# Routed experts behind a graph attention: the expert stage with its up part one block further ahead

## What is computed

```python
x = x + gnn(layernorm(x), adj, W, a)          # 4 heads, softmax over neighbours
t = layernorm(x)                              # 8192 tokens x 128
scores = t @ Wg.T + bg; top 2 of 8 experts, p = softmax of the two scores
for e in range(8):
    h = relu(t @ W1[e].T + b1[e])             # 128 -> 512
    y = h @ W2[e].T + b2[e]                   # 512 -> 128
    out = out + combine[..., e:e+1] * y       # combine holds p, zero elsewhere
x = x + out
```

## Time and profile before

| | us |
|---|---|
| median of 3 runs | 859.47 (856.22 to 861.64) |
| span of the profiled execution | 856.6 |
| busy over the span: TensorE, VectorE, ScalarE, GpSimd | 647.1, 601.7, 457.6, 429.5 |
| first load of expert rows | 526.0 |
| first and last writing of `ysb` | 539.1, 800.3 |
| first load of the combining part | 805.95 |

### The profile page before, as it was taken

The page is one execution under the profiler, slowest core; times in us unless marked ns, Lnnn a source line. Parts: engine busy times, 40 slices in busy tenths (PEclk is TensorE's granted clock), DMA queues, the critical chain, the costliest instruction groups (busy, mean ns, idle before and its releaser), DMA issues.

```text
span 856.6 us, 26610 instructions
## 1 busy us (share of the span) xinstructions
PE 647.1 (76%) x8094; PEld 499.3 (58%) x8163; DVE 601.7 (70%) x1709; ACT 457.6 (53%) x885; POOL 429.5 (50%) x436
## 2 busy tenths in 40 slices
PE   0659999889988898888998812888888888888200
PEld 0435777667666676666666711767766767767200
DVE  3835888887777977878777452677677676777365
ACT  0545566555655655456644111667666666766243
POOL 0011337665666656565566563466556556556300
PEclk9955999989888998889887765999999999999755
DMA  8711112220222112210000015222222222222388
GB/s 272 272 50 50 51 51 70 76 70 14 74 68 74 36 44 74 68 68 12 26 27 20 27 34 111 58 73 71 62 70 73 65 69 73 63 68 62 90 255 245
DMA packets 70462, 67.10 MB, mean 78 GB/s; under 512 B 7378, under 2 KB 54141, under 8 KB 70416
## 3 DMA queue, kind: packets, MB, share of 16 engines
q1 hardware_dynamic: 52064, 44.31, 17.4%
q0 software_dynamic: 8816, 17.46, 6.1%
q10 hardware_dynamic: 9536, 4.73, 2.0%
HBM read 44.16 MB, written 23.22 MB: 79 GB/s over the span
## 4 chain that ended last, share of the span: by engine, by line
PE 32%; DVE 25%; issue 17%; ACT 8%; POOL 7%; DMA 7%; DVEq 1%; SPq 1%; ACTq 1%; POOLq 0%
PE bank L1267 6%; DVE G L1007 5%; ACT G L612 5%; PE bank L1258 4%; PE bank L1113 4%; PE bank L1087 4%; POOL rs L433 3%; PE bank L1101 3%; DVE G L1005 3%; DVE nb L722 3%; DVE bs L713 2%; DMA adji<-expert_out 2%; ACT xn L536 2%; DMA out<-adji 2%; POOL expert_rows L442 2%
## 5 line engine op out<-in xcount | busy, mean ns | idle before, releaser
L506 POOL DMA_INDIRECT expert_out<-ysb,bidx x142 | 159.3, 1122 | 121.6 <-DVE ysb L1026 67.7
L612 ACT ACTIVATE G<-bank,b1s,sc 128x256 f32<-128x256 f32 x284 | 137.1, 562 | 49.5 <-PE bank L1258 47.1
L531 ACT ACTIVATE G<-bank,s2c 128x512 bf16<-128x512 f32 x192 | 128.9, 681 | 54.3 <-PE bank L1087 54.0
L442 POOL DMA_INDIRECT expert_rows<-rowt,idx x128 | 130.3, 1018 | 49.9 <-issue 49.3
L1113 PE MATMUL bank<-V,G 128*128 128x66 bf16 x3072 | 143.0, 199 | 0.0
L1113 PEld LDWEIGHTS bank<-V,G 128*128 128x128 bf16 x3072 | 121.8, 101 | 31.2 <-issue 30.1
L1258 PE MATMUL bank<-xt,W1h 128*128 128x256 f16 x852 | 107.4, 277 | 29.5 <-issue 17.0
L1267 PE MATMUL bank<-W2h,G 128*128 x1704 | 106.6, 219 | 16.0 <-DVE G L1007 16.0
L1267 PEld LDWEIGHTS bank<-W2h,G 128*128 128x128 f16 x1704 | 98.5, 97 | 25.9 <-issue 25.0
L1258 PEld LDWEIGHTS bank<-xt,W1h 128*128 x852 | 77.7, 99 | 51.4 <-issue 41.5
L1005 DVE CAST G<-G 128x1024 f16<-128x1024 f32 x71 | 53.4, 752 | 74.1 <-ACT G L612 74.0
(11 more groups left out here) (176 smaller groups left out, 1083.3 us busy)
## 6 DMA issues: line engine op xcount, KB each, us to landing
adji<-in_adj SPq DMA_DIRECT2D x16, 1024.0 KB, 5.1
xb<-expert_rows SPq DMA_DIRECT2D x71, 130.0 KB, 2.2
adji<-expert_out SPq DMA_DIRECT2D x32, 256.0 KB, 4.0
out<-adji ACTq DMA_DIRECT2D x16, 256.0 KB, 3.1
expert_out<-ysb,bidx POOLq DMA_INDIRECT x142, 2.4
G<-in_L_ffn_W SPq DMA_DIRECT2D x1, 2048.0 KB, 13.9
expert_rows<-rowt,idx POOLq DMA_INDIRECT x128, 2.4
xr<-in_x SPq DMA_DIRECT2D x1, 768.0 KB, 10.7
```

What stands on the lines that cost most here:

```text
L442: pool.indirect_dma_start(xs, bass.IndirectOffsetOnAxis(ap=idx[:, Z.p, k, j:j + 1], axis=0), rowt[:, Z.p, j, :], None).then_inc(scattered[ ...
L506: pool.indirect_dma_start(ybuf, bass.IndirectOffsetOnAxis(ap=bidx[:, B.q, t:t + 1], axis=0), ysb[:, B.q, t, :], None, bounds_check=2 * TOK ...
L531: act.activation(G[:, M.p, h, mt, :], zb[k % 2][:, :], ACT.Relu, bias=s2c[:, M.p, mt, h:h + 1]).then_inc(S["z_used"], 1)
L612: act.activation(h32[:, U.p, c, :], Up[U.p][c // 2][:, (c % 2) * BLK:(c % 2 + 1) * BLK], ACT.Relu, bias=b1s[:, bass.ds(ex * NC + c, 1)], s ...
```

## The change

The up part of block n+2 stands beside the down part of block n: in step s X = s+3, U = s+2 and Y = s. Five steps (-3 to 1) stand ahead of the loop. `hp` has four buffers in place of two, and `split` waits for the down matmuls of block U-4 in place of U-2. PE reads the expert number of block X between the up and the down matmuls and keeps three numbers; at the head of a loop pass it reads all three anew. `bidx`, `xb`, `ysb`, `xt`, `h32` and the waits on `back` stay as they are.

```diff
@@ -246,8 +246,8 @@
         padrow = sb("padrow", [P, BT, ROW])
 
         h32 = Gf[:, 0:2 * NC * BLK].rearrange("p (a c n) -> p a c n", a=2, c=NC)
-        hp = G[:, :, :, :, :].rearrange("p a h t n -> p (a h t n)")[:, 4 * NC * BLK:8 * NC * BLK] \
-            .bitcast(FP16).rearrange("p (a q c n) -> p a q c n", a=2, q=2, c=NC)
+        hp = G[:, :, :, :, :].rearrange("p a h t n -> p (a h t n)")[:, 4 * NC * BLK:12 * NC * BLK] \
+            .bitcast(FP16).rearrange("p (a q c n) -> p a q c n", a=4, q=2, c=NC)
         xb = sb("xb", [P, 4, BT, ROW])
         xt = sb("xt", [P, 2, 2, BLK], FP16)
         ysb = sb("ysb", [P, 4, BT, D])
@@ -341,8 +341,8 @@
                 at = lambda k: Batch(2 + u + k, i, STEPS)
                 at.first = u == 0
                 return at
-            for s in range(-2, 2):
-                body(fixed(s, s == -2))
+            for s in range(-3, 2):
+                body(fixed(s, s == -3))
             with eng.Fori(0, (BLOCKS - 4) // STEPS) as i:
                 for u in range(STEPS):
                     body(looped(u, i))
@@ -598,7 +598,7 @@
             slots(act, body, 18)
 
             def hidden(at):
-                X, U = at(2), at(1)
+                X, U = at(3), at(2)
                 if X:
                     act.wait_ge(S["bt_ready"], X.n + 1)
                     ge(act, S["up_ready"], (X.n - 1) * NC)
@@ -1000,14 +1000,14 @@
             def split(U):
 
                 dve.wait_ge(S["hid_ready"], U.n * NC + NC)
-                ge(dve, S["down_ready"], U.n - 1)
+                ge(dve, S["down_ready"], U.n - 3)
                 c = Chain(dve, S["split_steps"], 2, U.n)
-                c.did(dve.tensor_copy(hp[:, U.p, 0], h32[:, U.p]))
+                c.did(dve.tensor_copy(hp[:, U.q, 0], h32[:, U.p]))
                 c.wait()
-                c.did(dve.tensor_tensor(hp[:, U.p, 1], h32[:, U.p], hp[:, U.p, 0], ALU.subtract))
+                c.did(dve.tensor_tensor(hp[:, U.q, 1], h32[:, U.p], hp[:, U.q, 0], ALU.subtract))
 
             def work(at):
-                X, U, Y = at(2), at(1), at(0)
+                U, Y = at(2), at(0)
                 if U:
 
                     dve.wait_ge(ld_rows[U.q], U.f * 16 + 16)
@@ -1230,10 +1230,16 @@
                             largest(F)
             slots(pe, body, 18)
 
-            held = {}
+            held = []
+
+            def expert(B):
+                return pe.value_load(tab[0:1, 1, bass.ds(B.n, 1)], min_val=0, max_val=E - 1)
 
             def layers(at):
-                X, U, Y = at(2), at(1), at(0)
+
+                X, U, Y = at(3), at(2), at(0)
+                if at.first:
+                    held[:] = [expert(at(k)) if at(k) else None for k in range(3)]
                 if X:
                     pe.wait_ge(ld_rows[X.q], X.f * 16 + 16)
                     ge(pe, S["xt_ready"], X.n - 1)
@@ -1242,21 +1248,17 @@
                         for t in range(BT):
                             last = pe.transpose(XTp[X.p][:, q, t * P:(t + 1) * P], xv[:, t, q, :], identh[:, :])
                     last.then_inc(S["bt_ready"], 1)
-                if Y:
-
-                    ey = held.pop("e", None)
-                    if ey is None or at.first:
-                        ey = pe.value_load(tab[0:1, 1, bass.ds(Y.n, 1)], min_val=0, max_val=E - 1)
+                ey, ex = held[0], held[2]
                 if U:
                     pe.wait_ge(S["xt_ready"], U.n + 1)
                     ge(pe, S["hid_ready"], (U.n - 1) * NC)
-                    ex = held["e"] = pe.value_load(tab[0:1, 1, bass.ds(U.n, 1)], min_val=0, max_val=E - 1)
                     for c in range(NC):
                         o = Up[U.p][c // 2][:, (c % 2) * BLK:(c % 2 + 1) * BLK]
                         for n, (wq, xq) in enumerate(((0, 0), (0, 1), (1, 0))):
                             w = W1h[:, wq, bass.ds(ex, 1), c * P:(c + 1) * P].rearrange("p e h -> p (e h)")
                             last = mm(o, w, xt[:, U.p, xq, :], start=(n == 0), stop=(n == 2))
                         last.then_inc(S["up_ready"], 1)
+                held[:] = held[1:] + [expert(X) if X else None]
                 if Y:
                     pe.wait_ge(S["split_steps"], Y.n * 2 + 2)
                     ge(pe, S["y_ready"], Y.n - 1)
@@ -1264,7 +1266,7 @@
                         w = [W2h[:, q, bass.ds(ey, 1), c, :].rearrange("p e d -> p (e d)") for q in range(2)]
                         for n, (hq, wq) in enumerate(((0, 0), (1, 0), (0, 1))):
                             for t in range(BT):
-                                last = mm(Yp[Y.p][:, t, :], hp[:, Y.p, hq, c, t * P:(t + 1) * P], w[wq],
+                                last = mm(Yp[Y.p][:, t, :], hp[:, Y.q, hq, c, t * P:(t + 1) * P], w[wq],
                                           start=(c == 0 and n == 0 and t == 0),
                                           stop=(c == NC - 1 and n == 2), skip_group_check=True)
                     last.then_inc(S["down_ready"], 1)
```

## The result

| | before | after |
|---|---|---|
| median of seven runs each, us | 858.33 (854.81 to 861.64) | 864.36 (861.33 to 867.99) |
| ratio after / before | | 1.0082 (95%: 1.0050 to 1.0115) |
| span of the profiled execution | 856.6 | 862.2 |
| first load of expert rows | 526.00 | 523.45 |
| start of y(0), of y(68) | 539.09, 795.69 | 537.46, 798.11 |

The kernel became slower by 0.8%. That is inside the range and on the forecast side of no change, but within the 1% that I had called no change, so my likeliest case (871 us, slower by over 1%) did not come. It is the rival in which the collisions cost little.

The account below looks back on a forecast made before the run. It took a loop of waits over TensorE, ScalarE and VectorE as the bound, 3.77 us per block. Pairs at 7.8 us gave +8.6, filling +3.0, draining -0.1: span 868.1, median 871 us, range 854 to 884.5.

Parts of the forecast that it names:

- my likeliest case: Expert stage: cast and scatter collide in every step, a pair of blocks takes 7.7 to 8.0 us, 871 us; chance 0.50.
- the rival in which the collisions cost little: Expert stage: casts and scatters hardly stretch each other, a pair takes 7.2 to 7.7 us, 860 us; chance 0.30.
- The bound before, and the loop that the change cuts: Expert stage: a TensorE, ScalarE, VectorE loop sets 3.77 us per block; cutting it removes waits of 14.0 and 66.2 us.
- Where the stall goes: VectorE's L1016 waits for the scatter of block s-2, idle 0.5 to 1.0 us each step, 40 to 65 in total.
- The terms of the loop: From y through scatters, landing, reaction and VectorE's step to the next y but one: 7.47 us for two blocks.
- Collisions: VectorE's cast starts some 0.4 us into GpSimd's first scatter in every step, adding 0.33 us: 7.8 us a pair.
- The sum: Expert stage: 34 pairs at 7.8 us make 265.2 against 256.6, +8.6; with filling and draining +11.5 us.
- Filling and draining: Ends of the expert stage: one more step before y(0) costs 3.0 us; draining takes 9.65 us against 9.78.
- The rival that it does what it says: Expert stage: TensorE sets the pace at 3.51 us per block if landings are fast enough, 844.5 us; chance 0.07.

Follow-up runs that it names:

- the eight buffers: The changed kernel with eight buffers of `bidx` in place of four: 852.76 us, ratio 0.9950 to before.
- the kernel with registers: The changed kernel with eight buffers of `bidx` and TensorE's expert numbers in four fixed registers, second run, second chip: 882.11 us, ratio 0.9839 to before there.

## Why the prediction was right, and where it was not

**The bound before, and the loop that the change cuts.** Right. L1005's 66.2 us and the 14.0 us at L1267 are gone from after, and they come back in the eight buffers, where the relu is the last to be ready again.

**Where the stall goes.** Right, and shown from three sides: 67.4 us at L1016, none with eight buffers, none with `bidx` a step later, and 66.3 when the wait alone is put into before. I had said 40 to 65 us and 0.5 to 1.0 in each step. It is 1.96 us in every second step and none in the other.

**The terms of the loop.** Right. These came from rows of before, and after has them as follows (from the timeline above and the other pairs):

| | predicted | measured |
|---|---|---|
| end of y to first scatter | 0.87 | 0.88 |
| first to second scatter | 1.28 | 1.41 |
| second scatter to landing | 2.3 | 2.25 |
| reaction of VectorE | 0.15 | 0.2 |
| L1016 to end of y | 2.87 | 2.79 |
| sum | 7.47 | 7.53 |

**Collisions: the step that failed.** I added 0.33 us to each pair because I let the blocks follow each other evenly, one period apart, and so placed each cast 0.4 us into a first scatter. But the loop ties step s to step s-2 and nothing ties the odd steps to the even ones. VectorE's own order puts the prompt step right behind the late one, its y 2.78 us later, and then waits. That rhythm puts the casts at other places than I did, and there they cost less. The starts and durations of all casts and scatters in the two timelines show what a place costs:

| the cast starts | trace, example | cast (free: 0.69) | scatter (free: 0.98) |
|---|---|---|---|
| 0.21 before the scatter | before, 647.01 | 0.69 | 1.34 |
| 0.45 before the scatter | after, 654.39 | 0.69 | 1.10 |
| 0.12 into the scatter | before, 556.55 | 0.69 | 0.98 |
| 0.25 into the scatter | after, 659.15 | 0.69 | 1.06 |
| 0.50 into the scatter | before, 567.68 | 0.69 | 1.32 |
| 0.54 into the scatter | before, 658.16 | 0.96 | 0.98 |

In after nearly every cast overlaps a scatter, but almost always at the second and the fourth of these places. Only one of the casts, at 560.77 us, is stretched (0.92). Their mean is 697 ns, where it was 755 before. On the path of the loop only the first scatter's 1.10 in place of 0.98 is left, 0.12 us a pair and not 0.33. Even a cast 0.4 us into a scatter, where I had placed it, would by the fourth and fifth rows have cost the scatter and not itself. All this is read from the two traces: no run moves the phase by itself.

The Trainium skill (SBUF — State Buffer, section Who interferes with whom) gives an exclusive lock, so that the second of two such instructions waits for the first. For whole instructions the traces do not bear it out: in the last four rows the cast starts while the scatter runs and at most 0.27 us are lost by it or 0.34 by the scatter, and the kernel took 864 us where the prediction has 893 for a full wait. Read for parts of a scatter they do. In the first two rows of the table the scatter ends 1.55 us after the cast began, in both cases, as if its last 0.86 us had to wait for the cast's end. A cast that starts 0.54 to 0.79 us into one ends about 1.5 us after the scatter's start.

**The sum.** y(0) to y(68) took 4.05 us more, where 8.6 was forecast. Three parts make it:

- The first eight blocks took 33.57 us against 30.46, +3.1. There the pairs take 8.0 to 8.9 us, with landings up to 3.6 us after the start of the scatter.
- Block 56 took +1.7. In its trace GpSimd stands idle for 2.06 us between the two scatters of one block:

```profile
755.75 0.98 POOL L506 DMA_INDIRECT expert_out<-ysb,bidx  x1 [2.06 <-issue]
```

  Before has such a gap there too (its two scatters start 3.16 us apart, at 752.14 and 755.30) and shows no loss, since its wait had two periods to spare. In after it lies on the path and the pair takes 9.25.
- The other 29 pairs took 7.51 us, against 7.54 for two blocks before, -0.8 together.

So without the first eight blocks and block 56, neither of which stood in the sum, the 68 blocks would have gone a little faster than before. Both act through the loop that was forecast, but that the kernel came out slower and not even is owed to them, and to that extent the direction was luck.

**Filling and draining.** Filling cost 0.9 us and not 3.0. I had charged the added step in full. The first up part and the first cast, in before and then in after, show what came in its place:

```profile
530.67 2.74 PE L1258 MATMUL bank<-xt,W1h 128*128 128x256 f16 x12 [0.59 <-issue]
...
534.60 0.69 DVE L1005 CAST G<-G 128x1024 f16<-128x1024 f32 x1 [5.95 <-ACT G L612]
```

```profile
527.25 2.52 PE L1259 MATMUL bank<-xt,W1h 128*128 128x256 f16 x12
...
530.96 0.69 DVE L1005 CAST G<-G 128x1024 f16<-128x1024 f32 x1 [4.83 <-ACT G L612]
```

From this cast to y(0) it takes 4.5 us in before and 6.5 in after. The 2.0 us between them are the added step without a y of its own (2.87 - 0.48 = 2.39), less the 0.33 that before waits there for a relu. Against them the cast starts 7.5 us behind the first load of rows and not 8.6, since the up part starts 0.9 us sooner, without the 0.59 us of idle time in front of it, and takes 0.2 us less. Draining was 9.57 against the 9.65 of the prediction.

**The rival that it does what it says.** Its condition, a landing 4.0 us or less after y, did not come. But the run with the wait taken out shows that its price was wrong too: 852.8 us and not 844.5. The step without the head was right: 2.88 + 0.35 = 3.23 us forecast, 3.25 measured, the load before the down matmuls costing 0.22 to 0.31. The head of a pass costs 3.3 us and not 2.2, and 3.6 to 3.7 where the clock falls behind it. Hence 3.67 a block and not 3.51. In after the same heads (2.32 us idle at 661.36) lie beside the longer loop and cost nothing visible.

**The chances.** Little collision had 0.30 and the forecast 0.50. The phase was argued from one assumption and carried too much weight. What spoke for little collision holds for the whole stage: of the 134 scatters from 543 to 796 us, 73 take under 1.00 us. The measured 864.36 us lies between the 860 of the one and the 871 of the other. Given equal chances, the two would have carried the same weight.

## What to carry to other kernels

When a pipeline is made deeper, list every buffer that the moved stage touches, small index buffers too. A buffer count that stays the same brings its wait one step nearer. If that wait reaches back through a DMA's landing to something that stands behind it on the same engine, add the loop up: one such loop of 7.5 us over two steps ate all that the deeper pipeline had won. Either remedy took the wait away here: compute the index a step later, or give it twice the buffers.

Before placing a collision in time, ask what fixes the phase. Here the steps were tied only to the step before last, and they settled in pairs, not evenly.

## What the runs showed of the hardware

- Three register loads in a row at a loop head left TensorE idle for 2.3 us, and the granted clock was then 0.50 for about 3 us at five of seven such heads with eight buffers of `bidx` (at two it stayed at 1.00). Before, with two loads and 1.5 us of idle time, kept 1.00 at all of them.
- A cast and a scatter disturb each other by their phase: in 0.69 and 0.98 us of work, a cast that starts 0.12 us into the scatter costs nothing, and one 0.21 us before it costs the scatter 0.36 us.
- The gap of GpSimd between the two scatters of a block is 0.30 us, but at block 56 it is 1.8 to 2.2 us in all six traces of the first chip (1.81 in before, 2.06 in after). Its cause is open.
- On a second chip matmuls stalled three times in a row, 0.72 to 0.74 us apart, with no wait named (and in the kernel with registers no transfer of code near most of them), and the clock fell to 0.50 behind a third to a half of these places. Before took 896 and 915 us there, against 858. The cause is open.
- With passes of 32 steps one loop head left TensorE idle for 6.26 us, with eight packets of the kind "instruction" in the 10 us around it.
